# First cross attention: the row-sum matmul of a unit placed ahead of the last maxima of the unit behind it, and a start-up that uses both PSUM pairs in turn and makes the values in the score banks

## The reference, cut to what matters

```
b, l = 8, 256;  NH, CHD = 16, 8;  1601 context rows of 128
cq  = heads(ci @ cq_w, NH, CHD)                    # 8 x 16 x 256 x 8
ckv = encoder_outputs @ ckv_w                      # 8 x 1601 x 256
ck, cv = split(ckv); each to 8 x 16 x 1601 x 8
cctx = softmax(cq @ ck.T / sqrt(CHD)) @ cv         # no mask
hidden_states = hidden_states + cctx @ cdense_w
```

## Time and profile before

| | |
|---|---|
| median of 3 runs | 3704.31 us (3703.56 to 3713.9) |
| profiled execution | 3718.22 us, of which the span is 3716.4 us |
| PE busy over the span | 3439.8 us (93%) |
| first matmul of the phase | at 453.92 us |
| first step's first maximum, q = 7 | at 515.14 us |
| row sums of the phase, PE | from 539.1 to 1300.9 us |

### The profile page before, as it was taken

How to read it: one execution, slowest core, us unless ns; L and a number is a source line. 1 busy time by engine, 2 the same in 40 slices (tenths; PEclk the granted TensorE clock), 3 DMA queues, 4 the chain that set the end, 5 groups by cost and what they waited for, 6 DMA issues and landing times. The chain is left out here.

```text
span 3716.4 us, 74073 instructions
## 1 busy us (share of the span) xinstructions
PE 3439.8 (93%) x25048; PEld 2326.5 (63%) x25048; DVE 2020.9 (54%) x3324; ACT 1838.3 (49%) x3373; POOL 1589.8 (43%) x1421
## 2 busy tenths in 40 slices
PE   7788879898999979989999999999999998999997
PEld 5544634444444368875666666666666666888886
DVE  4454467777777644534555555555555553114454
ACT  2243336676676723334555555555555554333333
POOL 3211211121121101103777777777777776004554
PEclk9899879999999989997999999999999999999998
DMA  4764300000001032321010000010101001311200
GB/s 123 161 102 85 132 4 17 17 17 18 7 17 36 6 128 109 115 87 41 13 33 13 31 13 31 13 32 13 33 13 56 13 13 67 124 43 40 95 6 12
DMA packets 74750, 179.34 MB, mean 48 GB/s; under 512 B 14720, under 2 KB 44928, under 8 KB 68480
## 3 DMA queue, kind: packets, MB, share of 16 engines
q1 hardware_dynamic: 70240, 161.81, 14.5%
q0 software_dynamic: 4128, 12.60, 1.3%
HBM read 115.09 MB, written 59.26 MB: 47 GB/s over the span
## 5 line engine op out<-in xcount | busy, mean ns | idle before, releaser
L1624 POOL TENSOR_TENSOR cross_acc<-cross_acc,cross_probs 128x512 f32<-128x512 f32 (+1 forms) x704 | 920.8, 1308 | 160.8 <-ACT cross_probs L1687 119.5
L1687 ACT ACTIVATE cross_probs<-cross_s,cross_bias 128x512 f32<-128x512 f32 (+1 forms) x832 | 529.6, 684 | 489.9 <-PE cross_s L1906 488.1
L1783 DVE TENSOR_REDUCE cross_partmax<-cross_r 128x1 f32<-128x400 f32 (+1 forms) x1024 | 541.3, 570 | 347.0 <-PE cross_r L1876 328.7
L1243 DVE TENSOR_REDUCE cross_partmax<-cross_m 128x2 f32<-128x800 f32 (+1 forms) x512 | 497.9, 991 | 201.1 <-PE cross_m L1342 199.8
L1165 ACT ACTIVATE cross_probs<-cross_s 128x512 f32<-128x512 f32 (+1 forms) x832 | 452.2, 595 | 145.6 <-PE cross_s L1362 145.2
L1919 PE MATMUL cross_av<-cross_probs,cross_v 128*64 128x256 f32 (+1 forms) x3328 | 458.3, 393 | 0.0
L1919 PEld LDWEIGHTS cross_av<-cross_probs,cross_v 128*64 128x64 f32 (+1 forms) x3328 | 199.3, 136 | 172.5 <-ACT cross_probs L1687 75.9
L1104 POOL TENSOR_TENSOR cross_diag<-c_ident,cross_negmax 128x256 fp32r<-128x256 f32 x128 | 75.8, 613 | 484.0 <-DVE cross_negmax L1251 484.0
L1373 PE MATMUL cross_av<-cross_probs,cross_v 128*32 128x256 f32 (+1 forms) x3328 | 269.6, 396 | 12.3 <-ACT cross_probs L1165 9.5
L1342 PE MATMUL cross_m<-cross_ks,cross_qd 64*128 64x400 f32 (+1 forms) x1024 | 210.2, 415 | 51.1 <-DVE cross_partmax L1243 46.0
L1900 PE MATMUL cross_s<-cross_q_hi,cross_k_hi 64*128 64x256 f32 (+1 forms) x1664 | 253.8, 299 | 0.0
(11 more groups left out here) (301 smaller groups left out, 6601.0 us busy)
## 6 DMA issues: line engine op xcount, KB each, us to landing
d_masked_ctx<-tail_ctx_split SPq DMA_DIRECT2D x8, 1602.0 KB, 5.3
d_self_qk<-selfproj_qk_split POOLq DMA_DIRECT2D x32, 256.0 KB, 5.5
self_qs<-d_self_qk SPq DMA_DIRECT2D x64, 128.0 KB, 7.5
self_ks<-d_self_qk SPq DMA_DIRECT2D x64, 128.0 KB, 8.1
d_cross<-tail_pr SPq DMA_DIRECT2D x8, 1024.0 KB, 4.6
cross_qp<-d_cross SPq DMA_DIRECT2D x64, 128.0 KB, 2.4
d_cross<-cross_out SPq DMA_DIRECT2D x64, 128.0 KB, 1.8
tail_attn<-d_cross SPq DMA_DIRECT2D x8, 1024.0 KB, 5.5
```

The lines of the kernel that those rows point to most:

```text
L1243: nc.vector.tensor_reduce(partmax[:, :, jt // 2, jt % 2, i:i + 1], m_pair(M_SET[q], w), AX.X, ALU.max).then_inc(maxed, 1)
L1624: nc.gpsimd.tensor_tensor(acc[0:w, g % 2], left, probs[0:w, slot % NPB], ALU.add).then_inc(added, 1)
L1687: nc.scalar.activation(probs[0:w, (g * KT + t) % NPB], src_, ACT.Exp, scale=XHD ** -0.5, bias=bias[0:w, p, t:t + 1]).then_inc(probs_ready, 1)
L1783: nc.vector.tensor_reduce(partmax[:, m, i:i + 1], r_ps[MAX_BANK[q]][:, 0:KCH[i][1]], AX.X, ALU.max).then_inc(maxed, 1)
```

## The change

It has two parts.

In the step, the waits and the matmul of the row sum now stand ahead of q = 6 of the unit after, where there is such a unit: in 30 of the 32 units.

In the start-up, keys use pair 0 for chunks 0 and 1 and pair 1 for chunks 2 and 3 (`K_SET_AHEAD`). The values are made in the three score banks and the result bank, with a function of their own on PE and on ACT. Maxima take pair 0 and pair 1 in turn (`M_SET_AHEAD`), and wait for the one before the last. The keys of unit 1 move behind the maxima of unit 0, and the first scores move ahead of q = 1 of unit 1.

```
+M_SET_AHEAD = tuple(q % 2 for q in range(NM))
+K_SET_AHEAD = (0, 1)
 # ACT
 def ahead(u):
+    k_half x4 of u
+    for i in range(2):
+        act.wait_ge(vp_ready, i + 1 + PRIME)
+        first_values(2 * i)
+        first_values(2 * i + 1).then_inc(cv_ready, 1)
+    k_half x4 of following(u, NG)
 # DVE
+    k_half x4 of u
     for q in range(NM):
+        maxima(u, q, M_SET_AHEAD)
+        if q == 8:
+            negative_maxima(u, 0)
+    negative_maxima(u, 1)
+    k_half x4 of second
+    maxima(second, 0, M_SET_AHEAD)
     add_shift(u)
+    for q in range(1, 7):
+        maxima(second, q, M_SET_AHEAD)
 # PE
+def first_values(k):
+    bank = av_ps if k == 3 else s_ps[k]
+    for t in range(4 * k, min(4 * k + 4, KT)):
+        w = width(t)
+        last = nc.tensor.matmul(bank[0:w, t % 4 * C:(t % 4 + 1) * C], ct[:, 0, t * P:t * P + w], wv[:],
+                                start=True, stop=True)
+    if k % 2:
+        last.then_inc(vp_ready, 1)
 def ahead(u):
+    k_chunk x4 of u
+    for k in range(4):
+        first_values(k)
     for q in range(NM):
+        if q > 1:
+            pe.wait_ge(maxed, q - 1 + PRIME)
+        maxima(u, q, M_SET_AHEAD)
+    for i in range(2):
+        pe.wait_ge(maxed, NM - 1 + i + PRIME)
+        k_chunk x2 of second
+    maxima(second, 0, M_SET_AHEAD)
     shift(u)
+    pe.wait_ge(cv_ready, 2 + PRIME)
+    scores(tile(u, None, 0))
+    scores(tile(u, None, 1))
     for q in range(1, 7):
         if q == 1:
             pe.wait_ge(shifted, 1 + PRIME)
+        else:
+            pe.wait_ge(maxed, NM + q - 1 + PRIME)
+        maxima(second, q, M_SET_AHEAD)
+        if q == 3:
+            values(tile(u, None, 0))
 # PE, step
-        for q in later[first:]:
+        for q in later[first:] if t < KT else ():
             max_after_item(nxt, after, q)
     pe.wait_ge(av_copied, n + 1 + PRIME)
     ...
     nc.tensor.matmul(m_ps[SUM_SET][:, 0:S], c["sum8"][:], av[:], start=True, stop=True).then_inc(sum_ready, 1)
+    if after:
+        for q in max_after_at[KT]:
+            max_after_item(nxt, after, q)
```

More of the change, by code:

```diff
@@ L1134, in _, with k_half @@
                 act.wait_ge(v_set, 2)
-                def k_half(u, i, h):
+                def k_half(u, i, h, sets=K_SET):
                     b, p, g, n = u
@@ L1139, in k_half @@
                     act.wait_ge(k_ready, n * 4 + 2 * i + h - 3 + PRIME)
-                    nc.scalar.activation(k_high[:, i, h, 0:w], m_ps[K_SET[i]][:, h * 512:h * 512 + w], ACT.Identity,
+                    nc.scalar.activation(k_high[:, i, h, 0:w], m_ps[sets[i]][:, h * 512:h * 512 + w], ACT.Identity,
                                          scale=c["low"][:, 4:5], bias=c["low"][:, 2:3]).then_inc(k_high_ready, 1)
@@ L1197, in beside @@
                         values(nxt, 1)
+                def first_values(k):
+                    tiles = range(4 * k, min(4 * k + 4, KT))
+                    w = width(tiles[-1])
+                    bank = av_ps if k == 3 else s_ps[k]
+                    return nc.scalar.activation(
+                        v[0:w, 0, tiles[0]:tiles[-1] + 1, :, 0:CHD],
+                        bank[0:w, 0:len(tiles) * C].rearrange("p (t h d) -> p t h d", t=len(tiles), h=NH), ACT.Copy)
                 def ahead(u):
@@ L1201, in ahead @@
                         for h in range(2):
-                            k_half(u, i, h)
+                            k_half(u, i, h, K_SET_AHEAD)
+                    for i in range(2):
+                        act.wait_ge(vp_ready, i + 1 + PRIME)
+                        first_values(2 * i)
+                        first_values(2 * i + 1).then_inc(cv_ready, 1)
                     for i in range(2):
                         for h in range(2):
-                            k_half(following(u, NG), i, h)
-                    for i in range(2):
-                        values(u, i)
+                            k_half(following(u, NG), i, h, K_SET_AHEAD)
                     for r in range(2):
@@ L1289, in ahead @@
                     second = following(u, NG)
[L1290 to L1293, removed]
+                    for i in range(2):
+                        for h in range(2):
+                            k_half(u, i, h, K_SET_AHEAD)
                     for q in range(NM):
-                        maxima(u, q)
-                    for j in range(2):
-                        negative_maxima(u, j)
+                        maxima(u, q, M_SET_AHEAD)
+                        if q == 8:
+                            negative_maxima(u, 0)
+                    negative_maxima(u, 1)
+                    for i in range(2):
+                        for h in range(2):
+                            k_half(second, i, h, K_SET_AHEAD)
+                    maxima(second, 0, M_SET_AHEAD)
                     add_shift(u)
-                    for q in range(7):
-                        maxima(second, q)
+                    for q in range(1, 7):
+                        maxima(second, q, M_SET_AHEAD)
                 def step(u, nxt):
@@ L1311, in _, with k_chunk @@
                 pe.wait_ge(w_ready, 32)
-                def k_chunk(u, i, h):
+                def k_chunk(u, i, h, sets=K_SET):
                     b, p, g, n = u
@@ L1319, in k_chunk @@
                         pe.wait_ge(cl_ready, (b + 1) * NC + PRIME)
-                    o, cols, keys = m_ps[K_SET[i]][:, h * 512:h * 512 + w], slice(g * P, (g + 1) * P), slice(k0, k0 + w)
+                    o, cols, keys = m_ps[sets[i]][:, h * 512:h * 512 + w], slice(g * P, (g + 1) * P), slice(k0, k0 + w)
                     nc.tensor.matmul(o, wk_hi[:, cols], c_hi[:, p, keys], start=True, stop=False)
@@ L1331, in values_made, with maxima @@
                     last.then_inc(vp_ready, 1)
-                def maxima(u, q):
+                def maxima(u, q, sets=M_SET):
                     b, p, g, n = u
@@ L1341, in maxima @@
                     for r in range(2):
-                        last = nc.tensor.matmul(m_ps[M_SET[q]][:, r * 512:r * 512 + w], qd[ROWS[r], g, j, t * P:(t + 1) * P],
+                        last = nc.tensor.matmul(m_ps[sets[q]][:, r * 512:r * 512 + w], qd[ROWS[r], g, j, t * P:(t + 1) * P],
                                                 ks[ROWS[r], g, k0:k0 + w], start=True, stop=True)
@@ L1409, in ahead @@
                 def ahead(u):
-                    b, p, g, n = u
                     second = following(u, NG)
[L1412 to L1416, removed]
                     for i in range(2):
-                        pe.wait_ge(k_ready, 8 + PRIME)
-                        values_made(u, i)
+                        for h in range(2):
+                            k_chunk(u, i, h, K_SET_AHEAD)
@@ L1427, in ahead @@
+                    for i in range(2):
+                        pe.wait_ge(maxed, NM - 1 + i + PRIME)
+                        for h in range(2):
+                            k_chunk(second, i, h, K_SET_AHEAD)
+                    maxima(second, 0, M_SET_AHEAD)
                     shift(u)
-                    for q in range(7):
+                    pe.wait_ge(cv_ready, 2 + PRIME)
+                    scores(tile(u, None, 0))
+                    scores(tile(u, None, 1))
+                    for q in range(1, 7):
```

23 lines of the change are left out of this document (6 added, 17 removed).

## The result

| | before | after |
|---|---|---|
| median of 7 runs each | 3711.43 us (3703.56 to 3719.82) | 3681.43 us (3669.92 to 3689.98) |
| ratio after to before | | 0.9929, 95% interval 0.9908 to 0.9951 |
| profiled execution, span | 3716.4 us | 3673.2 us |
| phase's first matmul to q = 7 of the first step | 61.22 us | 39.02 us |
| an ordinary unit, row sum to row sum | 23.76 us | 23.74 us |

By the ratio the gain is 26 us on a base of 3711, and 18 to 34 us by its interval. The forecast was a gain of 22.1 us and a time of 3682.2. The two spans differ by 43 us, more than the ratio says.

The account below looks back on a forecast made before the run. Units were taken as close to PE's limit, the start-up as a chain of engines waiting for each other. Start-up 22.1 us plus nothing for the row sum: 3704.3 - 22.1 = 3682.2, range 3668 to 3693.

Parts of the forecast that it names:

- The start-up: Start-up of the phase: q = 7 of the first step written at 493.0 instead of 515.14, a gain of 22.1 us.
- keys of unit 1: Start-up: moved behind unit 0's maxima, PE may write their first chunks at 476.0, when q = 14 is taken.
- The rise of the clock: Start-up: clock rises 5.8 us, give or take 1.2, into PE's unbroken keys and values, at 459.7.
- the bounds of 20.1 to 25.7: Start-up gain: 20.1 us with PE at the low clock throughout, 25.7 with PE at 2.4 GHz throughout.
- The row sum: End of 30 units: sum ahead of q = 6 starts ACT's logarithm 1.27 us earlier but gains nothing.
- the round of pair 0: Unit's end: q = 6, 7, 8 each wait for DVE to take the one before, about 1.54 us a round.
- PE's slot of 0.63 us: Row sum's time on PE: with the cover gone, at most this in each of 30 units, 18.9 us.
- the saved slot: Rival, units: the sum's slot is saved too, up to 18.9 us more, 3663.3; chance 0.10, whole or over 3 us.
- its small form of a tenth of a microsecond a unit: Rival, units: only the small waits behind q = 7 shrink, giving 3 us.
- the pairs don't run in turn: Rival, start-up: rounds stay 1.79 us, 22 maxima lose 19.6 us, time 3701.8; chance 0.12, including other waits.
- The slower case: Rival, units: the sum makes q = 6 late; needs 0.74 us a unit beyond 0.26 spare to cancel 22.1; chance 0.04.
- the first steps: Rival, first units: clock rises 3 us later, losing 1.5 us, 3683.7; counted within the forecast.

Follow-up runs that it names:

- The run without the cover: Changed kernel with q = 7 written into pair 1 instead of pair 0: 3653.56 us, ratio 0.9860 to the kernel before.
- the start-up alone: Changed kernel with the old order of row sum and q = 6 put back in the step: 3682.53 us, ratio 0.9944 to before.
- the order alone: Kernel before with only the row sum moved ahead of q = 6, old start-up kept: 3700.17 us, ratio 0.9983 to before.
- the run with the maxima in series: Changed kernel whose start-up waits before each maximum until DVE has taken the one just before: 3693.74 us, a single run.
- sum twice: Changed kernel with the row-sum matmul issued twice in a row into the same place: 3690.14 us, ratio 0.9946 to before.

## Why the prediction was right

**The start-up.** Forecast from the first matmul to q = 7: 493.0 - 453.92 = 39.1 us. Measured 39.02 in the first profile, 37.9 to 39.0 in the six profiles in which the new start-up and the pair of q = 7 are unaltered, against 59.5 to 61.2 in four with the old one. The means are 38.4 and 60.5, a gain of 22.0 where 22.1 was forecast. The steps hold one by one, as distances from the first matmul: q = 0 at 7.7 forecast, 7.87 measured; keys of unit 1 at 22.1 and 22.15; first score at 30.5 and 30.1. The rise of the clock was put 5.8 us into the unbroken stretch, after the values of the trace before, and came at 5.7 in the first profile. That match is luck. In the other five of the six profiles it came 4.1 to 5.5 us behind the first matmul, three times before the 4.6 us that I had allowed for, and in the four profiles with the old start-up it came 2.8 to 5.9 us behind the start of the values. q = 0 stands at 7.1 to 7.9 us accordingly, which is most of the spread of 1.2 us in q = 7. All six lie inside the bounds of 20.1 to 25.7, taken off the mean of before.

**The row sum.** Costed at nothing because the round of pair 0 covers it. The units kept their length, the idle time split as forecast (about 0.3 and 0.8 forecast, 0.20 and 0.84 measured), and ACT's wait fell to 0.76 (0.8 forecast). The run without the cover gave 1.0 us a unit. Here the prediction was wrong: it held PE's slot of 0.63 us to be the most that could come out with the cover gone, but the release of the keys comes sooner too, 0.93 us between q = 6 and the first key chunk. Two more sizes were off, neither with weight: the slot is 0.53 and not 0.63, and units behind a batch's end are 0.15 us shorter (23.94 to 23.79, three of them in the phase), 0.5 us together. The last goes with the new start-up and not with the order: it is 23.74 to 23.80 us with the start-up alone and 23.95 to 23.97 with the order alone. Why, no run shows.

**The rivals.** That the saved slot is worth up to 18.9 us is refuted by the units of 23.74, and so is its small form of a tenth of a microsecond a unit. That the pairs don't run in turn is refuted by 9 and 7 maxima in line; its price of 19.6 us was put too high, since the run with the maxima in series lost 16.3. The slower case has its mechanism (sum twice), with 0.37 us of room. The Trainium skill ("TensorE: Matmul & The Clock Gate", section "A second HAM failure mode: psum-queue depth-cycling") says that idle times between groups of matmuls make the clock go back and forth. The trace agrees: up at 455.6, down at 462.4 among the maxima, and falls behind the ends of units. Among the maxima of the start-up it cost nothing, as forecast. In the units a fall costs 1.2 us, which I had looked for only in the first steps.

**The sum.** 22.1 us were forecast against 26 by the ratio, whose interval of 18 to 34 holds it. The median of three that the level was built on, 3704.3, lay below that of all seven runs of before, 3711.4, and near that of the 26 later ones, 3705.3. That 3681.4 came out so close to 3682.2 is in part luck: single runs of one kernel lie up to 30 us apart. The granted clock goes with them: in the 26 runs of before, the five fastest (3690.57 to 3693.76) had 0.967 to 0.971, the five slowest (3715.53 to 3720.45) 0.957 to 0.962.

## What to carry to other kernels

A wait that an engine gets rid of is worth what waits behind it: follow the released instruction to the next one that something else releases, here by a chain of pieces that share one buffer, and cost the move at zero when that chain is unchanged. When such a move gives nothing, look whether the chain can be broken now: the sum ahead and q = 7 in the other pair each left the unit as long as it was, and together they took 1.0 us off each unit, 25 us in all by the ratios. A start-up that runs once and alone deserves its own order: two buffers in turn, and keys that don't wait for their copies. And compare distances inside the phase that was changed: the rest of this program varies by 20 us from one execution to the next.

## What the runs showed of the hardware

The row sum, two rows of MATMUL of 256 columns in the trace, holds PE 0.53 us in front of a matmul pair of the maxima and 0.63 us in front of the scores. Sixteen maxima written at 1.2 GHz or 2.4 GHz went through DVE at the same 0.90 us each, as long as the pairs took turns; in one pair a round took 1.54 us at the full clock and 1.79 at the low one. The clock rose 4.1 to 5.7 us behind the start of the unbroken keys and values in six profiles of the new start-up, and 2.8 to 5.9 us behind the start of the unbroken values in four of the old one. The fall of the granted clock shown within a unit lasted 3.4 us and cost 1.2 us; over a whole execution the low clock summed to 302 us in the profile before and 224 us in the profile after, of which the start-up explains 29.
